# A bidirectional Mamba-2 layer with a feed-forward part on one core: tokens turned by VectorE and SBUF transfers, dt multiplied by GpSimd, half of the exponents bounded by VectorE

## What is computed

```python
zxbcdt = x @ Win                                   # 256 -> 512 (z), 640 (xs, B, C), 8 (dt)
xBC = silu(conv1d(xBC, convw, depth=4) + convb)
xs, Bm, Cm = split(xBC, [512, 576])                # 8 heads of 64, state of 64
dt = softplus(dt + dtb); A = -exp(Alog); dA = exp(dt * A)
def step(h, inp):
    dBx = einsum('bh,bn,bhp->bhpn', dt_t, B_t, x_t)
    h = dA_t[:, :, None, None] * h + dBx
    return h, einsum('bn,bhpn->bhp', C_t, h)
y = (scan(step) + Dsk * xs) * silu(z)
y = y * rsqrt(mean(y * y) + 1e-05) * normw @ Wout
...
x = x + concat([out_fwd, out_rev]) @ Wo + bo
x = x + layernorm(x) @ (W + C V_r)' + b
```

## Time and profile before

| | |
|---|---|
| median of 3 runs | 630.82 us (629.98 to 631.05) |
| profiled execution, span from first to last instruction | 629.0 us |
| one loop body (219.46 to 293.07) | 73.61 us |
| busy in that body: PE, DVE, ACT, POOL | 72.01, 61.99, 67.15, 52.45 us |

### The profile page before, as it was taken

One profiled execution on the slowest core, in us unless ns is written; L12 is line 12 of the kernel. 1 busy time (PEld: TensorE's weight loads), 2 busy tenths in 40 slices (PEclk: granted clock), 3 DMA queues, 4 the chain that ended last, 5 costly groups with the idle time before them and its releaser, 6 DMA issues.

```text
span 629.0 us, 13895 instructions
## 1 busy us (share of the span) xinstructions
PE 592.0 (94%) x4320; PEld 461.0 (73%) x4320; DVE 503.6 (80%) x991; ACT 547.2 (87%) x1197; POOL 409.4 (65%) x427
## 2 busy tenths in 40 slices
PE   1998999999999999999999999999999999999995
PEld 1776687777877777777877778777777777777784
DVE  2669788996979879797888969798797978879663
ACT  4689998979999899988999799897999989997952
POOL 1006948787486864878476874868648684768843
PEclk9999999999999999999999999999999999999997
DMA  7533514236061541418132360614416170343500
GB/s 220 189 109 115 198 40 124 92 106 203 8 200 27 171 114 41 169 28 255 28 116 95 107 204 0 211 25 160 126 28 182 26 241 12 92 122 99 181 1 33
DMA packets 43545, 70.71 MB, mean 112 GB/s; under 512 B 8000, under 2 KB 30592, under 8 KB 43520
## 3 DMA queue, kind: packets, MB, share of 16 engines
q1 hardware_dynamic: 43520, 70.40, 36.7%
HBM read 59.37 MB, written 4.72 MB: 102 GB/s over the span
## 4 chain that ended last, share of the span: by engine, by line
PE 55%; ACT 18%; DVE 13%; issue 8%; POOL 3%; SPq 1%; DMA 1%; DVEq 0%; ACTq 0%; POOLq 0%
PE mi L621 14%; ACT bs L968 8%; PE pj L487 7%; PE py L580 7%; PE pj L489 6%; PE pj L488 6%; DVE xc L1378 5%; PE mi L687 4%; PE py L598 3%; ACT bs L974 2%; ACT L953 2%; DVE bs L1405 2%; DVE ss L1437 2%; ACT xc L935 1%; DVE xres L1445 1%
## 5 line engine op out<-in xcount | busy, mean ns | idle before, releaser
L1378 DVE SCALAR_TENSOR_TENSOR xc<-pj,cw,xc 128x510 f32<-128x510 f32 (+2 forms) x240 | 175.4, 744 | 24.9 <-ACT xc L935 23.0
L968 ACT ACTIVATE bs<-bs,s_all 128x128 f32<-128x128 f32 x512 | 158.4, 388 | 0.2
L1892 POOL TENSOR_TENSOR yg<-yg,sz 128x512 f32<-128x512 f32 x60 | 76.9, 1287 | 81.6 <-DVE yg L1424 81.6
L487 PE MATMUL pj<-xnt_hi,w_hi 128*128 128x512 f32 x288 | 126.1, 438 | 0.9 <-DVE xc L1378 0.8
L489 PE MATMUL pj<-xnt_hi,w_lo 128*128 128x512 f32 x288 | 114.2, 396 | 0.0
L488 PE MATMUL pj<-xnt_lo,w_hi 128*128 128x512 f32 x288 | 113.8, 395 | 0.0
L621 PE MATMUL mi<-wc,yg 128*128 128x256 f32 x480 | 112.1, 386 | 0.8 <-DVE xres L1445 0.2
L621 PEld LDWEIGHTS mi<-wc,yg 128*128 128x128 f32 x480 | 88.6, 190 | 16.9 <-issue 3.3
L1405 DVE TENSOR_TENSOR bs<-bs,gm 128x512 f32<-128x512 f32 x128 | 86.1, 680 | 8.5 <-ACT bs L974 7.7
L1871 POOL TENSOR_TENSOR xw<-xdt,w_end 128x512 f32<-128x512 f32 x48 | 49.6, 1045 | 49.8 <-ACT w_end L953 40.9
L1390 DVE TENSOR_TENSOR xdt<-mi,dt 128x512 f32<-128x512 f32 x64 | 42.8, 688 | 44.6 <-PE mi L547 44.2
(11 more groups left out here) (149 smaller groups left out, 1021.6 us busy)
## 6 DMA issues: line engine op xcount, KB each, us to landing
bs<-rows_dram SPq DMA_DIRECT2D x64, 512.0 KB, 5.4
es<-rows_dram SPq DMA_DIRECT2D x128, 96.0 KB, 3.0
xres<-in_x SPq DMA_DIRECT2D x8, 512.0 KB, 3.6
cc<-bcm SPq DMA_DIRECT2D x32, 128.0 KB, 2.3
out<-ot SPq DMA_DIRECT2D x32, 128.0 KB, 3.4
xin<-in_x SPq DMA_DIRECT2D x7, 512.0 KB, 5.3
rows_dram<-s_rows SPq DMA_DIRECT2D x128, 4.0 KB
cz<-bcm SPq DMA_DIRECT2D x16, 128.0 KB, 2.4
```

Source lines behind the costliest of these rows:

```text
L487: pe.matmul(ps[:], hi(k), xnt_hi[:, k, :], start=(k == 0), stop=False)
L968: i = nc.scalar.activation(bs[:, h, Q * c:Q * c + Q], bs[:, h, Q * c:Q * c + Q], ACT.Relu, bias=s_all[:, d, 0, c, h:h + 1], scale=-1.0)
L1378: i = dve.scalar_tensor_tensor(xc[:, t, to], pj[bank][:, of], cw[:, d, t, KW - 1 - s:KW - s], xc[:, t, to], ALU.mult, ALU.add)
L1892: pool.tensor_tensor(yg[:, d, p, :], yg[:, d, p, :], sz[:, d, p, :], ALU.mult).then_inc(yg_ready, 1)
```

## The change

There are three changes and new orders.

1. **Tokens.** `x_tokens` and `b_tokens` go, with their PSUM banks, and so does `xdt`. In their place DVE transposes each of the five tiles (`bcm`, four of `xs`) in blocks of 32x32 into a tile `turned` (`turn`, one instruction of 128x512, written with a step of five elements). SP then moves the blocks with 16 DMAs per unit, each 32 partitions with four runs of 160 elements, into `tok` (`carry`), which has tokens on the partitions, and the five tiles interleaved. `tok` exists once, so a unit's DMAs wait until the last pair of the unit before has been through `intra` and `inter` (`pair_done`). PE's `intra` and `state` read their stationary operand from `tok` with a step of five elements. `xw` now lies in the memory of `turned`.
2. **dt.** The product with dt is made in place in `tok` by POOL (`step`, four instructions per unit, which wait for all 16 DMAs). `intra` of the first pair waits for all four.
3. **Bounds.** For heads 1, 3, 5, 7 DVE makes the bound (`floor`, four tensor_scalar instructions of 128x128, subtract and min), and ACT only for the others. The exponential of all heads stays on ACT.

```diff
+BY_VECTOR = (1, 3, 5, 7)
+BY_SCALAR = (0, 2, 4, 6)
...
-        xdt = sb("xdt", [P, NC, DI])
-        xw = sb("xw", [P, NC - 1, DI])
-        btok = sb("btok", [P, NC, NS])
+        turned = sb("turned", [P, BLK, NC, SQ * (1 + KI)])
+        xw = turned[:].rearrange("p b c r -> p (b c r)")[:, 0:(NC - 1) * DI].rearrange("p (j n) -> p j n", j=NC - 1)
+        tok = sb("tok", [P, NC, P, 1 + KI])
...
+            def carry(b, d):
+                sp.wait_ge(turn_ready, (1 + KI) * (2 * b + d + 1))
+                alone(sp)
+                pair_done(b, d, KI - 1)
+                for i in range(BLK):
+                    for q in range(BLK):
+                        sp.dma_start(tok[SQ * q:SQ * q + SQ, :, SQ * i:SQ * i + SQ, :].rearrange("p c r t -> p c (r t)"),
+                                     turned[SQ * i:SQ * i + SQ, q]).then_inc(tok_loaded[i], 16)
...
             def intra(b, d, p):
...
+                if p == 0:
+                    pe.wait_ge(step_ready, NC * (u + 1))
...
-                        pe.matmul(py[bank][HP * half:HP * half + HP, Q * c:Q * c + Q], xdt[:, c, HP * h:HP * h + HP],
+                        pe.matmul(py[bank][HP * half:HP * half + HP, Q * c:Q * c + Q], tok[:, c, HP * half:HP * half + HP, p],
...
+            def turn(b, d, t):
...
+                dve.transpose(turned[:].rearrange("p b c (r t) -> p c b r t", t=1 + KI)[:, :, :, :, t],
+                              xs[:, d, t, :] if t < KI else bcm[:, d, :]).then_inc(turn_ready, 1)
...
+            def floor(b, d, h):
...
+                for c in range(NC):
+                    own = bs[:, h, Q * c:Q * c + Q]
+                    i = dve.tensor_scalar(own, own, s_all[:, d, 0, c, h:h + 1], 0.0, ALU.subtract, ALU.min)
+                i.then_inc(floored, 1)
...
+            def step(b, d, j):
...
+                own = tok[:, c, :, 0:KI].rearrange("p (z q) t -> p z t q", z=2)
+                i = pool.tensor_tensor(own, own, dt[:, d, c, :].rearrange("p (t z) -> p z t", z=2).unsqueeze(3).broadcast_to([P, 2, KI, HP]),
+                                        ALU.mult)
+                i.then_inc(step_ready, 1)
```

More of the change, by code:

```diff
@@ L567, in state @@
                     mm = pe.matmul(ps[LANES[half], 0:DI // 2].rearrange("p (s z q) -> p s z q", z=2, q=HP),
-                                   btok[:, ORDER[d][j], :], heads[:, :, MEMBERS[half], :], start=True, stop=True, skip_group_check=True)
+                                   tok[:, ORDER[d][j], 0:NS, KI], heads[:, :, MEMBERS[half], :], start=True, stop=True, skip_group_check=True)
                 mm.then_inc(full, 1)
@@ new lines, in forward_scan @@
+                weights(phase, it, b, 0, 3)
+                weights(phase, it, b, 0, 4)
+                if ahead:
+                    norm1_aggr(b + 1, 3)
+                state(phase, it, b, 0, 1)
+                mix(phase, it, last, 1, 0)
+                mix(phase, it, last, 1, 1)
+                weights(phase, it, b, 0, 5)
+                floor(b, 0, 7)
+                state(phase, it, b, 0, 2)
+                conv(b, 1, 2, 2)
+                norm2_bn(phase, it, last, 0)
+                s_copy(phase, it, 1)
@@ L1706, in forward_scan @@
+                conv(b, 1, 2, 3)
                 outputs(b, 0, 0)
-                norm2_bn(phase, it, last, 0)
-                weights(phase, it, b, 0, 4)
-                conv(b, 1, 1, 2)
-                conv(b, 1, 1, 3)
+                norm2_aggr(last, 0)
                 norm2_bn(phase, it, last, 1)
+                outputs(b, 0, 1)
+                weights(phase, it, b, 0, 6)
+                norm2_aggr(last, 1)
+                weights(phase, it, b, 0, 7)
+                turn(b, 1, 4)
```

801 lines of the change are left out of this document (391 added, 410 removed).

## The result

The changed kernel takes 778.1 us (median of 4 runs, 775.5 to 781.5) where the kernel before takes 630.4 (629.9 to 631.1): ratio 1.235, 95% interval [1.230, 1.239]. It is 148 us slower. Medians are of undisturbed executions throughout.

A forecast was written before the change was run, and what follows sets the result against it. PE was taken as nearly full (72.0 of a 73.6 us body), DVE fullest afterwards. Stretches 20.3, 12.5, 25.7 and 12.4 made a body of 70.9; seven bodies saved 19, ends added 6, giving 618 us, range 600 to 665.

The forecast's parts named there:

- The issue on SP: SP's 16 token DMAs per unit, taken at 0.40 us each, 6.4 us per unit, with ends 4.7 and 9.4.
- A: Loop-body stretch from a reversed unit's last `inter` to the next unit's first `intra`: forecast 20.3 us, before 16.0.
- C: Loop-body stretch from that next unit's last `inter` to the following reversed unit's first `intra`: forecast 25.7 us, before 24.9.
- SP is too slow: Rival: token DMAs issue at 0.59 us like `cc`, each chain grows 3.0, body 77.0, time 661 us; chance 0.20.
- Behind the 16 DMAs: SP's queue in A: loads of the second to fourth pair land 6 us later, still ahead of their pairs.
- From POOL's start to the first `intra`: End of A: four `step` and two `decayed_x`, 7.0 us, plus some 1.8 of other POOL work.
- The floors: DVE's 32 new tensor_scalar instructions per body, taken at 0.20 us each, 6.4 us.
- the floors collide with POOL: Rival: floors wait for POOL instructions in flight; body about 75, or 89 and 742 us if each waits; chance 0.10.
- DVE's transpositions: Ten new 128x512 transposes per body on DVE, taken at 0.69 us each, 6.9 us; range 3.5 to 13.8.
- POOL at 1.17: POOL's `step` and `decayed_x` with a 20-byte step, taken at 1.17 us each; far end 1.52.
- B and D: Stretches from first `intra` to last `inter`: next unit (B) 12.5 us, before 19.7; reversed unit (D) 12.4, before 12.9.
- The ends: Start and end of the kernel, less work to cover the chain: 3 us added for each, bounds 0 to 8.7.

The follow-up runs named there:

- run 5: Changed kernel with 4 copies per scan over all 128 partitions in place of the 16 transfers, block exchange left out: 747.2 us.
- run 1: Changed kernel with the bounds of heads 1, 3, 5, 7 back on ScalarE, no floors on VectorE: 756.3 us, ratio to before 1.203.
- run 4: Changed kernel with each floor as a scalar_tensor_tensor against a column of zeros in place of the tensor_scalar: 788.4 us.
- run 11: Kernel before, with floors of heads 1, 3, 5, 7 on VectorE as a minimum that also writes its accumulator, subtraction in ScalarE's exponential: 678.3 us, ratio 1.077.
- run 17: Kernel before, with only `wd` altered to read its first operand from PSUM in place of SBUF: 631.6 us, ratio 1.0020.
- run 12: Changed kernel with its floors as a minimum that also writes its accumulator, subtraction in ScalarE's exponential: 764.4 us.
- run 14: Changed kernel with four copies per scan in place of 16 transfers, and floors as a minimum that also writes its accumulator: 674.5 us, ratio 1.069.
- run 7: Changed kernel with four copies per scan, all bounds on ScalarE and every 20-byte step made dense, values left permuted: 652.6 us, ratio 1.040.
- run 8: Changed kernel with only VectorE's block transpositions writing densely, in runs of 32, values left permuted: 758.9 us.
- run 15: Changed kernel with four copies and all bounds on ScalarE, GpSimd's product with dt left out but for one element each: 672.9 us.
- run 13: Kernel before, plus 256 VectorE tensor_scalar instructions on constants that nobody waits for, all bounds on ScalarE: 678.2 us, ratio 1.077.
- run 18: Changed kernel with four copies and all bounds on ScalarE, GpSimd's products with dt moved ahead in its order: 678.7 us, ratio 1.077.

## Why the prediction was wrong

*What bounds the kernel, and what leaves the engines.* Right for ACT, which fell to 54.4 us per body (forecast 53.4), and near for POOL, 64.8 (62.6). Wrong for PE: it is busy 73.8 us per body for the 65.8 forecast, a part of it at half clock.

*The issue on SP.* The term failed: 0.60 for 0.40, 10.35 us per scan for 6.4 (an issue starts 0.64 us after the one before), 4.0 us in A and in C. This was the rival "SP is too slow", and its row, `cc` at 0.590 from SBUF to SBUF, was the right one: run 5 has 0.60 also for 128 partitions and 2560 B in a row. The rival's price (body 77.0) was too low, since it counted nothing behind SP.

*Behind the 16 DMAs.* This step failed: "they land 6 us later, still ahead of their pairs". The loads were early enough for PE, but not for DVE, where the floor of the second pair stands ahead of the sum of squares. It is the wait of 5.17 us in A, and behind it wait the mean square, the `mix` and the last two products. I had asked what was queued behind the new wait on SP, and not what was queued behind the floor's wait on DVE. Run 1, which has no floors, prices the strand: A is 1.7 us shorter without it.

*From POOL's start to the first `intra`.* The larger part of A's excess is here, and the prediction has no term for it. It went by POOL's chain alone, 8.8 us, where A needed 13.5. PE's two `state` and two `mix` ahead of the first `intra` were left out, and so was what PE's wait does to its clock: I had PE idle for some 5 us and still took a `mix` at 1.87. At full speed these four would take about 5.1 us (estimate: 0.70 for a `state`, as at 336.57, and 1.87 for a `mix`), and with the 3.9 us up to the first `state` (322.00 to 325.89) that gives 9.0: the forecast's 8.8 would have come out near by luck, over another chain. In run 1 they take 7.9 us (231.32 to 239.25), and A's excess behind POOL's start is 3.0; here the wait of 1.41 for the sum of squares comes to it, and the excess is 4.7. In C, 13 matmuls between 273.92 and 279.54 take 5.6 us, 2.5 more than at 0.23 apart; the chain of waits runs through them and on through DVE to its sum of squares.

*The floors.* The term failed by a factor: 0.48 for 0.20. 256 floors took 123.7 us, so 15.5 per body for 6.4. The mechanism was the rival "the floors collide with POOL", whose chance of 0.10 was too low: `wd` stood in the rows, and I took "no row has a tensor_scalar that met a long product" as a reason for the cheap end. Runs 4, 11 and 17 show the exclusion, from both sides: two forms that stretch, two that don't. Floors that aren't stretched gave 14 us behind the transfers and 73 without them (runs 12, 14), net of what that form costs.

*DVE's transpositions.* 1.13 for 0.69: 4.4 us per body, within my far end. L1305, from which I argued that a step costs nothing, reads with a step from PSUM; it says nothing of a write with a step into SBUF. Runs 7 and 8 show 0.685 when the write is dense. The transfers start later, at least in part by it: 3.9 us for 2.8 in A and 7.8 for 5.1 in C.

*POOL at 1.17.* 1.33, so 0.16 x 14, 2.2 us per body, a mis-sized term of little weight: with cheap transfers nothing is gained without the product (run 15). The weight loads with the same step showed as the prediction's sign had it: 32 matmuls of `intra` take 2.12 us (294.04) for 1.92.

*The sum.* A: start +1.1, issue +4.0, landing -0.5, behind it +4.7, together 9.3. C: +2.7, +4.0, -0.5, +5.9, together 12.1; the 5.9 are the products, 9.2 for 8.2, and POOL's two waits for DVE, 4.9. B and D are together 0.6 shorter than forecast. That makes the 20.8 us by which this body is longer (91.7 for 70.9). With the mean of 90.8, seven bodies give 139 of the 160 us between 618 and 778.

*The floor's cost on a DVE of 62 in 73.6.* The forecast let DVE's work grow to 69.8 of 70.9 and said that it "isn't over the limit". Run 13 shows what that is worth: work for which nobody waits costs 49 us per 66 on a DVE that was 80% busy.

*The ends.* Not told apart from the rest.

What stays open: with cheap copies and no floors the kernel is 39 us above the one before. 16 of these are the steps of 20 bytes (run 7). The other 23 are neither the length of GpSimd's product (run 15) nor, by the order tried, its place (run 18). I don't know whose they are. And no version here beats the kernel before: the token path with nothing left out reaches 756 at best.

## What to carry to other kernels

Take two suspected costs away together before calling either small: each of the two bounds looked worth 20 to 30 us while the other stood, and together they were worth 109. When an edit moves work to an engine, ask whether its instruction competes with a neighbour for SBUF (here a plain tensor_scalar within SBUF, or two SBUF inputs, beside a busy GpSimd), and what stands behind it in that engine's queue when its data come late. Sixteen small transfers on one queue cost 16 issues, whatever their size, and everything behind them in the queue comes as much later. And where a change makes TensorE wait some us, price the matmuls behind the wait at the lower clock, and look in its queue for what stands ahead of the one that you expect next.
